# A two-layer transformer on eight cores: weight conversion taken out of the first stage and put ahead of it, and the query of the next head computed one head early

## The reference

```python
x = _layernorm(x + attn0(x)); x = _layernorm(x + ffn0(x))
x = _layernorm(x + attn1(x)); x = _layernorm(x + ffn1(x))

# attn0, 16 heads of 128, T = 8192
q    = rmsnorm(apply_partial_rope(h @ w_qc @ w_qup, cos, sin), q_norm_w)
sw_k = apply_partial_rope(rmsnorm(h @ k_proj_w, k_norm_w), cos, sin); sw_v = h @ v_proj_w
kc   = compress(h, idx_c_w, idx_c_wz, ...)      # one row for every 16 positions
skv  = rmsnorm(compress(h, kvc_w, kvc_wz, ...)) # the 64 best of 512 per query, by kc
out0 = (softmax(q skv) skv + softmax(window 256: q sw_k) sw_v) group_w final_w
# attn1, 16 heads of 128 over 4 key heads, window 1024
q = rope(x @ wq); q = q / (norm(q) + EPS) * gamma_q       # k the same
out1 = softmax(q k / sqrt(D), within the window) v  @ wo
# ffn0: a dense product and the best 2 of 8 rank-8 experts
# ffn1: twice, 6 experts of 2048 -> 1024 -> 1024 -> 2048, all used, and a shared one
```

## Time and profile before

| | us |
|---|---|
| two runs | 24500.73 and 24593.12, median 24546.93 |
| the profiled execution | 24663.21 |
| its span on the slowest core (first to last instruction) | 24661.7 |
| spans of the eight cores | 24271.6 to 24661.7 |
| P0 with the pump | 330 to 3671 |

### The profile page before, as it was taken

One profiled execution on the slowest core, in us unless ns is written; L12 is line 12 of the kernel. 1 busy time (PEld: TensorE's weight loads), 2 busy tenths in 40 slices (PEclk: granted clock), 3 DMA queues, 4 the chain that ended last, 5 costly groups with the idle time before them and its releaser, 6 DMA issues.

```text
span 24661.7 us, 174647 instructions; the slowest of 8 cores (24271.6 to 24661.7 us)
## 1 busy us (share of the span) xinstructions
PE 11657.5 (47%) x44056; PEld 4932.6 (20%) x44056; DVE 6154.2 (25%) x11172; ACT 5011.4 (20%) x11129; POOL 1032.4 (4%) x1919
## 2 busy tenths in 40 slices
PE   0000013433434233343444444444468988897878
PEld 0000001111112111111111212121223333333333
DVE  0000014343333433324323333333321010001111
ACT  0111112213132231312211313131311111111111
POOL 0111110000000000000000000000000000000000
PEclk8555555555656556565566555655567777788989
DMA  2544540000101001010011010101023333333433
GB/s 72 145 145 156 143 137 7 26 29 3 52 3 39 16 8 47 3 52 3 26 60 43 1 39 1 39 1 39 1 66 111 111 110 114 115 113 109 123 121 118
DMA packets 1219564, 1569.06 MB, mean 64 GB/s; under 512 B 161640, under 2 KB 1044781, under 8 KB 1218350
## 3 DMA queue, kind: packets, MB, share of 16 engines
q1 hardware_dynamic: 1076174, 1101.10, 14.7%
q0 software_dynamic: 142432, 456.80, 6.3%
HBM read 1385.53 MB, written 171.97 MB: 63 GB/s over the span
## 4 chain that ended last, share of the span: by engine, by line
PE 43%; DVE 19%; ACT 12%; DMA 11%; issue 11%; POOL 1%; DVEq 1%; ACTq 1%; SPq 0%; POOLq 0%; PEldq 0%
PE bank L243 29%; PE bank L1266 2%; DVE p_msc L1316 2%; DMA xl<-hT_full 2%; PE bank L380 2%; ACT p_pT L1270 1%; PE bank L1803 1%; DVE p_ncol L1320 1%; DMA xl<-hT_loc 1%; PE bank L359 1%; DVE a_rows L368 1%; ACT a_msc0p L1870 1%; DVE p_rows L374 1%; PE bank L1276 1%; ACT a_grp L676 1%
## 5 line engine op out<-in xcount | busy, mean ns | idle before, releaser
L243 PE MATMUL bank<-p_xsl,slabC 128*128 128x512 bf16 x8192 | 2066.8, 422 | 54.9 <-ACT p_wbsb L945 47.1
L1266 PE MATMUL bank<-ident_f_sb,p_msc 128*128 128x128 f32 x2304 | 904.3, 441 | 1466.7 <-ACT p_pT L1270 1448.7
L243 PE MATMUL bank<-p_hh,slabC 128*128 128x512 bf16 x6144 | 1505.3, 414 | 76.3 <-DVE p_hh L958 75.8
L1793 PE MATMUL bank<-ident_f_sb,a_msc0p 128*128 128x128 f32 x1536 | 557.0, 434 | 1973.3 <-ACT a_pT L1797 1947.9
L243 PE MATMUL bank<-a_hbf,kvc_w_bf 128*128 128x512 bf16 x256 | 111.6, 436 | 2432.6 <-DVE a_hbf L340 2432.6
L243 PEld LDWEIGHTS bank<-p_xsl,slabC 128*128 128x128 bf16 x8192 | 866.1, 106 | 1249.1 <-issue 833.7
L340 DVE CAST a_hbf<-xl 128x512 bf16<-128x512 f32 x464 | 198.9, 429 | 2869.7 <-DMA xl<-hT_full 1846.1
L243 PE MATMUL bank<-p_hn,slabC 128*128 128x512 bf16 x3072 | 808.0, 433 | 162.7 <-ACT p_hn L897 162.7
L243 PEld LDWEIGHTS bank<-p_hh,slabC 128*128 128x128 bf16 x6144 | 641.0, 104 | 935.8 <-issue 615.5
L1266 PEld LDWEIGHTS bank<-ident_f_sb,p_msc 128*128 128x128 f32 x2304 | 411.7, 192 | 1980.5 <-issue 1980.5
L1793 PEld LDWEIGHTS bank<-ident_f_sb,a_msc0p 128*128 128x128 f32 x1536 | 315.3, 206 | 2328.1 <-issue 2294.7
(11 more groups left out here) (365 smaller groups left out, 17266.6 us busy)
## 6 DMA issues: line engine op xcount, KB each, us to landing
slabC<-WupB SPq DMA_DIRECT2D x768, 256.0 KB, 2.8
slabC<-WdnB SPq DMA_DIRECT2D x768, 256.0 KB, 2.9
slabC<-WswB SPq DMA_DIRECT2D x384, 256.0 KB, 2.8
xl<-hT_full POOLq DMA_DIRECT2D x256, 256.0 KB, 3.1
slabC<-WsuB SPq DMA_DIRECT2D x256, 256.0 KB, 2.8
slabC<-WsdB SPq DMA_DIRECT2D x256, 256.0 KB, 2.7
xl<-hT_loc POOLq DMA_DIRECT2D x208, 256.0 KB, 3.1
slabA<-finB SPq DMA_DIRECT2D x192, 256.0 KB, 3.4
```

The costliest lines, as they stand in the source:

```text
L243: s=(kci == 0), p=(kci == nk - 1): e.matmul(o, l, r, start=s, stop=p),
L1266: P.op("tensor", lambda e, i9=i9, bnk=bnk, pp=pp: e.transpose(bnk[:, 0:128], msc[:, pp * 1152 + i9 * 128: pp * 1152 + (i9 + 1) * 128], sb[ ...
L1793: P.op("tensor", lambda e, i4=i4, bnk=bnk, pp=pp: e.transpose(bnk[:, 0:128], msc0[:, pp * 512 + i4 * 128: pp * 512 + (i4 + 1) * 128], sb[" ...
```

## The change

Three parts.

1. The class WconvPump and its calls are gone. In its place `emit_wconv` runs ahead of P0, before P0's tiles are allocated: for each 128 rows of each matrix, over their whole width (512, 1024 or 2048), POOL issues the load (it waits for the cast four jobs back), DVE casts, SP issues the store. There are 364 jobs: 148 of width 2048, 152 of 1024, 64 of 512. At the end POOL and SP wait for the last stores, and P0's loads come behind that.
2. P1: the query gemm of head h is emitted ahead of the four query tiles of head h-1, rope_norm of head h behind them. Banks 6 and 0 and the tiles qbf and dqT take turns.
3. rope_norm gets a parameter `lookback`: its first waits look at the counter of its matmuls so many steps back. P2 passes 2 and alternates between two sets of scratch tiles and of banks (5, 6 and 4, 7). The second to fourth query gemm of P2 waits for the first vv of the last rope only.

```diff
@@ rope_norm
-    P.wait("vector", rn0)
-    P.wait("scalar", rn0)
+    P.wait("vector", rn0, max(0, rn0.val - lookback))
+    P.wait("scalar", rn0, max(0, rn0.val - lookback))
@@ emit_p2, keys and queries alike
+                p_ = fl % 2
-                          Ss=Sbuf[:, 0:512], qs=ro_qs, tmp=ro_t, sq=sqs,
-                          rows=rows, scalemat=smat, out_bf=dst,
+                          Ss=Sbuf[:, 0:512],
+                          qs=(ro_qs, ro_qs2)[p_], tmp=(ro_t, ro_t2)[p_],
+                          sq=(sqs, sqs2)[p_], rows=(rows, rows2)[p_],
+                          scalemat=(smat, smat2)[p_], out_bf=dst,
-                          statbank=banks[5], bcbank=banks[6], vv=vv, ev=ev)
+                          statbank=(banks[5], banks[4])[p_],
+                          bcbank=(banks[6], banks[7])[p_], vv=vv, ev=ev, lookback=2)
+            vvc = P.ctr("vv")
+            pre = ([tok(ev), tok(vv)] if qtr == 0
+                   else [(vvc, vvc.val - 2)])
             gemm(P, f"p2q{sr}{qtr}", chunks=chunks, ftiles=fts, N=512,
                  banks=banks[0:4], evac=ev_q, evac_eng="vector",
-                 pre_toks=[tok(ev), tok(vv)])
+                 pre_toks=pre)
@@ emit_p0p1
-        if wsm is not None:
-            wsm.pump(23)
@@ heads of P1
+        for h in range(P1_LIM["h"]):
+            pq = h % 2
+            bank_q = (banks[6], banks[0])[pq]
...
+            pre = [q_srctok[pq]] if q_srctok[pq] else [tok(ev), tok(vv)]
+            cm = gemm(P, f"aq{r}{h}", chunks=chunks, ftiles=[0], N=512, banks=[bank_q],
+                      evac=None, pre_toks=pre)
+            emit_qt_loop(pend_h[0])
+            P.wait_tok("vector", [cm])
+            scc = P.ctr("sc")
+            P.wait("vector", scc, max(0, scc.val - 4))
+            rope_norm(P, sb, banks, src=bank_q[:, 0:512], Cs=Cb[:, 0:512], Ss=Sb[:, 0:512],
+                      qs=qs0, tmp=rot0, sq=sq0, rows=rows, scalemat=smat0,
+                      out_bf=(qbf, dqT)[pq][:, 0:512], wrow=sb["qnrow_sb"],
+                      eps_col=rms_col, extra_scale=1.0, half=32, N=512,
+                      statbank=banks[5], bcbank=banks[7], vv=vv, ev=ev)
+            vvc = P.ctr("vv")
+            q_srctok[pq] = (vvc, vvc.val - 2)
+            pend_h[0] = {"h": h, "pq": pq, "qtok": tok(vv)}
+        emit_qt_loop(pend_h[0])
@@ build_fused
+                emit_wconv(P, wctx, jobs, wcd)
+                P.wait("sync", wcd)
...
-            emit_p0p1(P, actx, io, sb, banks, bp, ws, jobs)
+            emit_p0p1(P, actx, io, sb, banks, bp, ws, None)
```

More of the change, by code:

```diff
@@ L1630, in emit_p0p1 @@
         c0 = c * 512
-        if wsm is not None:
-            wsm.pump(22)
         load_cs0(c0)
@@ L1670, in emit_p0p1 @@
     P.barrier()
-    if wsm is not None:
-        wsm.finish()
     for r in range(P1_LIM["sr"]):
@@ L1828, in emit_p0p1, with emit_qt_loop @@
         it = [0]
-        for h in range(P1_LIM["h"]):
-            chunks = []
-            for kc in range(4):
-                ch_ = ws.chunk(qupB, kc * 128, h * 128, 128,
-                               row1=((kc + 1) * 128 if kc % 2 == 0 else None))
-                ch_["lcols"] = lambda fl, ft: 0
-                ch_["rhs"] = qcT[:, kc * 512: kc * 512 + 512]
-                chunks.append(ch_)
-            cm = gemm(P, f"aq{r}{h}", chunks=chunks, ftiles=[0], N=512, banks=[banks[6]],
-                      evac=None, pre_toks=[tok(ev), tok(vv)])
-            P.wait_tok("vector", [cm])
-            P.wait("vector", P.ctr("sc"))
-            rope_norm(P, sb, banks, src=banks[6][:, 0:512], Cs=Cb[:, 0:512], Ss=Sb[:, 0:512],
-                      qs=qs0, tmp=rot0, sq=sq0, rows=rows, scalemat=smat0,
-                      out_bf=qbf[:, 0:512], wrow=sb["qnrow_sb"], eps_col=rms_col,
-                      extra_scale=1.0, half=32, N=512, statbank=banks[5], bcbank=banks[7],
-                      vv=vv, ev=ev)
-            mask_tok[0] = mask_tok[0] + [tok(vv)]
+        pend_h = [None]
+        q_srctok = {0: None, 1: None}
+        def emit_qt_loop(pdh):
+            if pdh is None:
+                return
+            h, pq = pdh["h"], pdh["pq"]
+            mask_tok[0] = mask_tok[0] + [pdh["qtok"]]
             for qt in range(4):
@@ L1900, in emit_p0p1 @@
                 it[0] += 1
+        for h in range(P1_LIM["h"]):
+            pq = h % 2
+            bank_q = (banks[6], banks[0])[pq]
+            chunks = []
+            for kc in range(4):
+                ch_ = ws.chunk(qupB, kc * 128, h * 128, 128,
+                               row1=((kc + 1) * 128 if kc % 2 == 0 else None))
+                ch_["lcols"] = lambda fl, ft: 0
+                ch_["rhs"] = qcT[:, kc * 512: kc * 512 + 512]
+                chunks.append(ch_)
+            pre = [q_srctok[pq]] if q_srctok[pq] else [tok(ev), tok(vv)]
[14 more added lines that the diff above has]
+        emit_qt_loop(pend_h[0])
+        pend_h[0] = None
         emit_tail(pend[0])
```

105 lines of the change are left out of this document (33 added, 72 removed).

## The result

Median 23209.5 us (22888.85 to 23652.52, 11 runs) against 24517.57 us of the kernel before in the same runs (24443.58 to 24818.92, 10 runs). Ratio 0.9421, 95% interval 0.9371 to 0.947, taken from the undisturbed runs of both kernels alone, where the medians of all runs would give 0.9466: 1420 us less, faster. The forecast was 23490, in a range of 23130 to 23970. The forecast's gain was 1062 us, so a quarter of what was gained isn't in it.

The account below looks back on a forecast made before the run. P0 was taken as bound by a chain of short waits, P1 by a chain between heads. Gains of 573 (conversion), 465 (P1 heads) and 24 (P2) sum to 1062 us, giving 23490 us, range 23130 to 23970.

Parts of the forecast that it names:

- What bounds the kernel: P0, 3341 us: a chain of short waits, two chunks in flight, no engine full; conversion costs 1971 us of it.
- The conversion's rate: Conversion ahead of P0: 377.5 MB at 270 GB/s takes 1398 us, a gain of 573 us.
- The rival of a fast conversion: Conversion: longer rows bring 340 GB/s, 1110 us, total 23200; chance 0.14.
- The bound of 381 GB/s: Conversion's fast end, from the single 1 MB load: 991 us, gain 980 us.
- Depth: Conversion: each load waits only for the cast four back, so about three loads are outstanding during a cast.
- The rest of P0: P0 without conversion: 16 slices of 55.7 us, seven of 64.9 us and small additions, 1370 us stay.
- the two additions: P0: 4 us for the first loads and 20 us, an estimate, for the normalization between the two loops.
- Heads of P1: P1 head boundaries: earlier query gemm saves 5.3 us for 90 heads, 477 us, net 465 us.
- The 0.15 us charged for the gemm behind the broadcast: P1, per head: the 1.86 us gemm does not quite fit the 1.76 us gap before the next scores.
- the second set of scratch: P2 ropes: costed at nothing, period stays 15.2 us; the rival that half overlaps gave 669 us, chance 0.01.
- The two places of the Trainium skill: Conversion: about 358 GB/s a core would give 1054 us; descriptor writing held at casts would add 331 us.
- Slower: Conversion: load, cast and store do not overlap, 3439 us, total 25530; chance 0.04.

Follow-up runs that it names:

- the width-1024 run: Changed kernel with no conversion job wider than 1024 columns, which halves the rows of the 2048-wide jobs; single time 23950.43 us.
- the old pump with whole rows: Kernel before, its pump run ahead of P0 with chunks up to 2048 columns wide, so no rows are cut; median of three 24629.93 us.

## Why the prediction was off, point by point

- **What bounds the kernel.** Right: P0 was a chain of short waits with no full engine, and the conversion was the largest term in it. But it was not the place that paid: the old pump moved ahead of P0 made P0 end 177 us later. The ring and the whole rows brought the 836 us, and with the loads deepened the place beside P0 is the better one (1901 against 2827).
- **The conversion's rate: the step that failed.** "Divided by the share: 276, 281 and 274 GB/s ... I take 270". Measured 319 GB/s at a share of 0.99, 1184 us in place of 1398: 214 us. The three stretches had, for the most part, chunks that take half of each row, and the change makes all rows whole; the width-1024 run and the old pump with whole rows show it. Of the 214 us, 66 are what cut rows cost in the ring itself (1250 us). The other 148 lie between that ring's 302 GB/s and the forecast's 270: cut rows cost the old pump more, 281 against 318. There the two halves of a row went to two queues, one after the other, in the ring all left halves went first and through one; no run separates these, and the cause stays open. The neighbouring stretches of the same trace, with whole rows, would have given 324 to 334, that is 1130 to 1165 us. The rival of a fast conversion ("longer rows") had the right cause in part, and its total of 23200 is close to what was measured by luck: its own rate (340) was too high, and terms that it doesn't have made up for it. The bound of 381 GB/s, from one load alone, is no rate of a stage: over 1000 us no core in any run here moved more than 329, over 100 us up to 351, and only over 25 us over 400.
- **The range.** Its low end, 23130, was said to be conversion at about 325 GB/s. It isn't: 377.5/325 is 1162 us, 236 less than 1398, which gives 23254. 23130 takes 1038 us or 364 GB/s. The measured rate alone would have put the time at 23490 - 214 = 23276, inside the range; it takes the terms below to bring it to the edge.
- **Depth.** "about three loads are outstanding while one is cast" was enough: the share is 0.99 with four buffers and 0.82 with two.
- **The rest of P0.** 1370 us were forecast, 1300 measured (873 and 427). A slice of hT_loc takes 61.0 us and not 64.9. The 64.9 came from the last slice, beside which the pump's last chunks still ran: from its first load's issue to its last cast 38.0 us (3607.3 to 3645.3), and 33.9 in the changed kernel (2763.6 to 2797.6). 27 us are this, 19 that a slice of hT_full takes 54.6 with the normalization in it and not 55.7 without, 24 the two additions.
- **Heads of P1.** 465 forecast, 476 by the stage, 474 alone; the square 5.45 us nearer, as worked out. The 0.15 us charged for the gemm behind the broadcast was too much: 3.82 us from broadcast to scores on the mean of the 84, and 3.80 before, 0.02. Right.
- **P2.** 24 forecast, 27 to 31 measured by the stage. The boundaries themselves save 2.0 us each, 25 in all, as forecast; where the few others lie is not shown. That the second set of scratch saves nothing by itself agrees with the period of the ropes, 11995.79 - 11980.63 = 15.16 us from stat to stat, and 15.16 in the earlier trace rows.
- **P3.** No edit, no effect, but 570 us between cores of one run. It moves most of all stages, and the intervals of the ratios here are one to four per cent wide.
- **The two places of the Trainium skill.** The page "DMA: Bandwidth & Descriptors" of the Trainium skill (section on measured bandwidth) would have given, as an estimate, 1054 us for the conversion; measured 1184 (319 to 320 GB/s on each of the eight cores, at a share of 0.98 to 0.99), so the forecast of 1398 was farther off than the page. The page "SBUF — State Buffer" of the Trainium skill (section on the doors) says that a fast VectorE copy shuts GpSimd out from writing descriptors, which the prediction put at up to 331 us. Moving the casts to ScalarE changed the conversion by 0 us, and the load issues kept their median of 0.527 us. The trace shows no such cost here.
- **Slower.** The ring overlaps; the conversion is 1276 us away from the 2460 at which that rival decided.

In sum: 214 (rate), 70 (rest of P0), 11 (heads) and 7 (P2) stand on top of the forecast's 1062, that is 1364. Less 9 us by which the conversion begins later (338.8 for 329.8) and 12 between the profiled cores and the mean, it is the 1343 of above, within 1299 to 1542.

## What to carry to other kernels

GB/s divided by the DMA share does give the rate of full DMA engines to about 5% (315 to 336 from shares of 0.47 to 0.90, against 319 to 325), if it is taken from some hundred microseconds of chunks of the same shape as those to come: look up which job a stretch belongs to before dividing. Where a stage's length differs by some tens of microseconds, take PE's busy time out of it before calling the difference the change's. And a conversion that fills the DMA engines needn't stand ahead of the work that doesn't: what made it slow beside P0 was its two chunks in flight (the faster pump also moved all to one queue, and these weren't taken apart) and P0's two buffers, and with both deepened the two stages took 1561 us (340 to 1901) in place of 2488 one after the other.
